# Graph units: the second group's denominator rows are issued ahead of the stacking for the unit two on

## The reference

```python
nodes = {-1: inputs}                       # normalised x, 4 x 1024 x 128
for c in range(6):
    nsrc = min(c + 1, 5)
    ...
    q = ew[c, 0] * (nodes[in_q] @ We[eq] + be[eq])
    k = ew[c, 1] * (nodes[in_k] @ We[ek] + be[ek])
    v = ew[c, 2] * (nodes[in_v] @ We[ev] + be[ev])
    o = _mha(q, k, v, Wq[c], Wk[c], Wv[c], Wo[c])   # 8 heads of 16, softmax over 1024 keys
    nodes[c] = act_w[c] * o + q
return _layernorm(nodes[5], ln_g, ln_b)
```

## Time and profile before

| | |
|---|---|
| median of 3 runs | 3431.9 us (3427.04 to 3450.86) |
| profiled execution, its own time | 3439.62 us |
| its span, first to last instruction | 3437.8 us |
| mean granted TensorE clock | 0.922 |
| busy: PE, DVE, ACT | 3055.6, 2418.9, 2157.1 us |
| graph stage in the span | from about 1054 to 3360 us |
| a unit of the graph | about 96 to 104 us |

### The profile page before, as it was taken

The page is one execution under the profiler, slowest core; times in us unless marked ns, Lnnn a source line. Parts: engine busy times, 40 slices in busy tenths (PEclk is TensorE's granted clock), DMA queues, the critical chain, the costliest instruction groups (busy, mean ns, idle before and its releaser), DMA issues. The chain is left out here.

```text
span 3437.8 us, 49190 instructions
## 1 busy us (share of the span) xinstructions
PE 3055.6 (89%) x19007; PEld 1349.5 (39%) x19007; DVE 2418.9 (70%) x3094; ACT 2157.1 (63%) x2695; POOL 390.2 (11%) x330
## 2 busy tenths in 40 slices
PE   5698989899388999999999999999999999999994
PEld 4355555556123333333333333333333333333331
DVE  6655555552268877778887787878887777888853
ACT  1155555556225777767777677777777767777783
POOL 0000000000100111111111110111111111111013
PEclk9699999999658999989999899999999999999997
DMA  6000000000432434334443344444434433443302
GB/s 164 16 11 11 16 4 23 1 20 5 109 83 55 102 88 88 77 85 83 103 103 92 82 81 93 92 82 104 102 89 83 82 85 81 104 100 88 66 21 82
DMA packets 144224, 245.09 MB, mean 71 GB/s; under 512 B 56482, under 2 KB 92726, under 8 KB 140918
## 3 DMA queue, kind: packets, MB, share of 16 engines
q1 hardware_dynamic: 143414, 239.85, 31.4%
q10 hardware_dynamic: 576, 2.10, 0.2%
HBM read 165.00 MB, written 74.10 MB: 70 GB/s over the span
## 5 line engine op out<-in xcount | busy, mean ns | idle before, releaser
L1435 ACT ACTIVATE pt_b<-ps_max 128x1024 f32<-128x1024 f32 x1516 | 1497.1, 1025 | 536.2 <-PE ps_max L1286 531.5
L1468 DVE TENSOR_REDUCE mx_b<-ps_pair 128x2 f32<-128x1024 f32 (+1 forms) x1032 | 1245.6, 1207 | 250.9 <-PE ps_pair L1272 244.3
L1322 PE MATMUL ps_ctx<-pt_b,vs 128*32 128x512 f32 x6144 | 868.8, 639 | 3.8 <-ACT c_b L1424 3.5
L1468 DVE TENSOR_REDUCE mx_b<-ps_misc 128x1 f32<-128x512 f32 x1032 | 707.1, 685 | 207.0 <-PE ps_misc L1272 190.8
L1286 PE MATMUL ps_max<-qs,ks 50*128 50x512 f32 x3032 | 836.0, 456 | 3.6 <-DMA qs<-mpart 3.1
L1272 PE MATMUL ps_pair<-ks,qs 48*128 48x512 f32 x2040 | 574.3, 486 | 128.0 <-DVE mx_b L1468 99.3
L1272 PE MATMUL ps_misc<-ks,qs 48*128 48x512 f32 x1032 | 490.9, 476 | 58.9 <-DVE mx_b L1468 52.3
L1286 PEld LDWEIGHTS ps_max<-qs,ks 50*128 50x128 f32 x3032 | 388.3, 196 | 363.2 <-ACT pt_b L1435 226.7
L1272 PEld LDWEIGHTS ps_pair<-ks,qs 48*128 48x128 f32 x2040 | 239.4, 197 | 455.0 <-DVE mx_b L1468 378.4
L1272 PEld LDWEIGHTS ps_misc<-ks,qs 48*128 48x128 f32 x1032 | 203.8, 197 | 418.3 <-DVE mx_b L1468 335.3
L775 ACT ACTIVATE pt<-ps_max,cb 128x512 f32<-128x512 f32 x342 | 215.7, 685 | 237.0 <-PE ps_max L652 181.1
(11 more groups left out here) (181 smaller groups left out, 2375.5 us busy)
## 6 DMA issues: line engine op xcount, KB each, us to landing
partd<-part SPq DMA_DIRECT2D x24, 2048.0 KB, 9.1
qs<-partd SPq DMA_DIRECT2D x288, 128.0 KB, 5.7
ks<-partd SPq DMA_DIRECT2D x288, 128.0 KB, 6.8
xq<-node SPq DMA_DIRECT2D x24, 512.0 KB, 3.8
xk<-node SPq DMA_DIRECT2D x24, 512.0 KB, 4.8
xv<-node SPq DMA_DIRECT2D x24, 512.0 KB, 5.5
xf<-node SPq DMA_DIRECT2D x24, 512.0 KB, 4.7
node<-nt_b SPq DMA_DIRECT2D x48, 256.0 KB, 2.2
```

Of the source, the lines that this page charges most:

```text
L1322: ins = pe.matmul(psO[SLOT * i:SLOT * i + SLOT, :], vs[u % 2][:, kb, QUAD * (s // HALF_STEPS) + i], pt[:, (QUAD * S + i) % ENTRIES], start ...
L1435: act.activation(pt[:, e:e + 2].rearrange("p k n -> p (k n)"), at[:], ACT.Exp, scale=SCALE_B).then_inc(exp_done, 1)
L1468: nc.vector.tensor_reduce(mx2[:, at:at + n], (psP, psX)[p % 2][:, 0:CHUNK * n].rearrange("p (h n) -> p h n", h=n), AX.X, ALU.max).then_inc ...
```

## The change

In `unit(u)` of SyncE's program, `rows_of(NG * u + 1)` (the four denominator transfers of the second group) is called ahead of `stack(u + 2, 0)` instead of behind it. The calls and their waits are the same. The file grows by one line, so that what stands behind this place has line numbers one higher.

```diff
                     if u < LAST:
                         spread(NG * u)
+                    if u < LAST:
+                        rows_of(NG * u + 1)
                     if u < LAST - 1:
                         stack(u + 2, 0)
                     if u < LAST:
-                        rows_of(NG * u + 1)
                         spread(NG * u + 1)
                         maxima_rows(u + 1, 0)
                         rows_of(NG * u + 2)
```

## The result

The changed kernel takes 3322.2 us (median of 4 runs, 3309.56 to 3333.32), against 3437.7 (median of 4, 3427.04 to 3450.86). The ratio is 0.9661, with a 95% interval of 0.9601 to 0.9721: 3.4% faster. The profiled execution took 3333.3 us, with a span of 3331.5, and is one of the two longer of the four runs (3309.6, 3311.1, and twice 3333.3).

What follows compares the result with a forecast made beforehand. TensorE was taken to set the pace, stalled where VectorE waits for the second group's denominators. From the profiled 3439.6 us, 53.4 for the stall and 78.1 for the clock were subtracted, giving 3308.1 us; range 3290 to 3350.

Steps and rivals of the forecast that it cites:

- Step 1: Second reciprocal, units 1 to 21: denominator transfers ahead of the stacking remove VectorE's 2.54 us wait each, -53.4 us.
- Step 2: Second-to-third reciprocal distances, units 1 to 21: without the stall TensorE's clock no longer falls, -78.1 us (bounds 0 and 78.1).
- Step 3: SyncE's stacking starts 5.4 us later, but is first read some 30 us behind: cost 0.
- the forecast sum: Whole change: 53.4 us for the stall and 78.1 us for the clock, 131.5 us gained.
- Step 4: SyncE's queue behind the stacking: `rec_b` later, third group's rows 1.1 us late, hidden with 4.5 us to spare: cost 0.
- The rival of a wait moved to the third reciprocal: A slower stacking drain makes VectorE wait at the third reciprocal; 3510 us at 10 us more drain; chance 0.05.
- The clock rule beside the row: Skill's ramp penalty below 1% of the span: clock gain at most 34 us, time 3352; set aside for the distances' 78.
- the second term: The clock's part of the gain in units 1 to 21, -78.1 us.
- the sentence on the spread of the runs: If clock falls make the runs differ (3427 to 3451), the changed kernel has none and needs no correction towards the median.

Runs made afterwards that it cites:

- Experiment 1: Kernel before, transfers in the old order, with only VectorE's reciprocal of each unit's second group moved three rounds later: 3322.0 us, ratio 0.9687.
- Experiment 2: Changed kernel plus five chained VectorE fills ahead of the second reciprocal of units 1 to 21: 3495.0 us, ratio 1.0193 to the kernel before.
- Experiment 6: Changed kernel plus nine chained VectorE fills ahead of the second reciprocal of units 1 to 21: 3532.9 us, ratio 1.0315 to the kernel before.
- Experiment 3: Changed kernel plus five chained VectorE fills ahead of the fourth reciprocal of units 1 to 21: 3642.5 us, ratio 1.0656 to the kernel before.
- Experiment 4: Changed kernel with the second group's whole spread (inverses out, broadcast back) also ahead of the stacking: 3305.1 us, ratio 0.9664 to the kernel before.
- Experiment 7: Changed kernel plus one unread TensorE product behind each of the 47 maxima pieces ahead of unit 0: 3302.2 us, ratio 0.9669 to the kernel before.

## Why the prediction was right, step by step

**Step 1, the stall.** Forecast -53.4 us. The idle time is gone in all 21 units, and the first distance fell from a mean of 26.11 to 23.49, which makes 55. The guess of 4 us for issue and landing was not needed in its size: 9.4 us were in hand. Experiment 1 took the waits away as well, with the old order of transfers.

**Step 2, the clock.** Forecast -78.1. The second distances now sum to 432.2 us, against 510.7: -78.5. Experiments 2 and 6 show the cause, which was only argued from unit 22: delays of VectorE alone, without a wait for a transfer, bring the falls back. The argument itself was weaker than it read. All 21 units had the stall and five of them no fall, so the distances alone could not tie the one to the other. Unit 22 is a control for the clock (1.00), but not for the distance: without a stall its second distance is 21.99 before and 22.01 after, not 20.60, since its rounds differ. And the page's digits show the clock below 9 in three slices of the graph stage (13, 18 and 23), not in many; it was the distances that showed the loss. One thing remains that step 2 did not foresee: a single fall in unit 4, between the third and fourth reciprocals (a distance of 23.91), in a stretch without such a stall (from 1523 to 1540 us, TensorE's longest idle time there for VectorE is 0.50).

```profile
1530.00:1550.00 20.00, 19.12 (x94) 6.95 (x90) 15.19 (x19) 12.40 (x17) 3.01 (x3) 0.83 0.77 162
```

It cost 3.0 us. Experiments 3, 4, 6 and 7 had one or a few longer third distances of the same kind (27.05 where 24.20 is usual, 22.63, 25.42 and 22.50 at the most); what brings them on is open.

**Step 3, the later stacking.** Forecast 0, and it is 0: the stretch from unit 1 on fell by 131.5 us, the forecast sum. That it agrees to the tenth is chance: the two terms came to 55.1 + 78.5 = 133.6, and the fall in unit 4 took 3.0 back. Experiment 4 delayed the stacking by a further 10.4 us for nothing.

**Step 4, what stands behind the stacking.** `rec_b` 7.5 us behind the reciprocal was forecast, 6.8 is measured; the third group's rows 1.1 us late, 0.15 measured; its reciprocal waits nowhere. The rival of a wait moved to the third reciprocal did not happen, and no run here brought it about.

**The clock rule beside the row.** The figure of the Trainium skill (TensorE: Matmul & The Clock Gate, What's actually happening), below 1% of the span for the ramp, would have given 34 us for the second term. The trace shows 78. That figure is given there for the ramp at the start of a kernel; here the clock fell in 16 of the 21 units.

**The level.** 3308.1 was forecast, the median is 3322.2. The sum holds for the part of the program that it was about. What was wrong is the sentence on the spread of the runs, that the changed kernel would have none: its four runs spread by 23.8 us, as the four before did (23.8). In the profiles the kernels differ most ahead of unit 1: its first reciprocal comes at 1154.85 us in experiment 1's profile, at 1175.63 in experiment 4's and at 1200.50 in the changed kernel's, with the clock at 0.67 over 92 us of unit 0 in the last. The profile before had 1175.28, and 1175.28 + 2131.0 is a span of 3306.3, so the forecast met the two shorter runs (spans of 3307.8 and 3309.2). That the start of unit 1 in the one profile before lay in the middle of what the profiles show is luck. How long TensorE stays at 1.2 GHz after the change of stage differs between the profiles. That it also makes the spread between runs of one kernel is likely but not shown: the changed kernel's two shorter runs have a mean clock of 0.949 and the two longer 0.938, but only one of them has a profile. Why it differs is open.

## What to carry to other kernels

Where one engine feeds the busiest one, look for waits that recur at one place of the loop, and measure the distances between recurring instructions on both sides of them: the distance behind the wait showed more loss (78 us) than the wait (53). In a queue that issues in program order, a transfer that is small and soon needed goes ahead of a large one with time in hand, even if the large one is ready first and has to wait a little. The same gain was to be had by letting the consumer come three rounds later, which needs no change in the queue (experiment 1).

## What the runs showed of the hardware

TensorE's clock has two levels in these traces, 1.2 and 2.4 GHz. A stall of VectorE, TensorE's feeder, of 1.8 to 3.4 us was followed by a fall in 16 of 21 units, one of 3.3 us in all 21, one of 1.3 us in none. In unit 8 of the kernel before, the low level lasted 20.4 us, in a window of 30 us in which TensorE was busy for 28.16. The cost of a fall didn't grow with the stall, 5.0 us behind one of 3.3 and 5.1 behind one of 5.9. It did depend on the place: 10.8 us behind the fourth reciprocal, where the low level lasted some 23 us a unit and not 14. And around the start of unit 0, in experiment 7, TensorE was busy for 9.44, 8.51 and 9.65 us of three windows of 10, and the granted clock in each was 0.50.
